# A four-layer graph stack on one core: last normalisation and squares moved to ScalarE, a bias on GpSimd, all orders written anew

## What is computed

```python
# layer 0: one-head attention, e = leaky_relu(s_i + t_j), softmax over neighbours, relu
# layer 1: eight heads of 16 features, e times a weight made of adj, softmax over neighbours, elu
# layer 2: mean over neighbours @ rel_weights[1] + x @ self_w.T + self_b, layernorm with gamma and beta, relu
# layer 3: four heads of 32 features, attention of Wh with itself
Wh = jnp.einsum('bsf,hfd->bhsd', features, W)
scores = jnp.einsum('bhsd,bhtd->bhst', Wh, Wh) / jnp.sqrt(jnp.float32(D))
scores = jnp.where(adj_matrix[:, None, :, :] > 0, scores, NEG_INF)
attn = jax.nn.softmax(scores, axis=-1)
h = jnp.einsum('bhst,bhtd->bhsd', attn, Wh)
# and the last step of the whole
x = _layernorm(x + _L3_gnn_ref(x, adj, L3_gnn_W), axis=-1)
```

## Time and profile before

| | us |
|---|---|
| median of 3 runs | 2479.86 (2475.13 to 2485.67) |
| profiled execution | 2479.01 |
| its span | 2477.2 |
| TensorE busy | 2241.7 (90%) |
| VectorE busy | 2223.9 (90%) |
| ScalarE busy | 1940.5 (78%) |
| GpSimd busy | 230.2 (9%) |

### The profile page before, as it was taken

How to read it: one execution, slowest core, us unless ns; L and a number is a source line. 1 busy time by engine, 2 the same in 40 slices (tenths; PEclk the granted TensorE clock), 3 DMA queues, 4 the chain that set the end, 5 groups by cost and what they waited for, 6 DMA issues and landing times.

```text
span 2477.2 us, 56662 instructions
## 1 busy us (share of the span) xinstructions
PE 2241.7 (90%) x23629; PEld 1505.8 (61%) x23629; DVE 2223.9 (90%) x4194; ACT 1940.5 (78%) x2152; POOL 230.2 (9%) x136
## 2 busy tenths in 40 slices
PE   4668999999999999999999999999999999998966
PEld 3567566575756657585665757566575756657331
DVE  3898899999999999999999999999999999999756
ACT  2758798787889878788987878798787979877724
POOL 0001010010101001010010101001010100101010
PEclk9789999999999999999999999999999999999979
DMA  7348034442614445251544525154452614405030
GB/s 132 88 90 163 13 96 86 109 98 69 112 48 125 86 103 104 69 112 44 129 86 103 104 67 114 44 129 86 96 111 54 125 45 126 90 27 95 10 60 9
DMA packets 262911, 214.20 MB, mean 86 GB/s; under 512 B 137664, under 2 KB 239168, under 8 KB 261696
## 3 DMA queue, kind: packets, MB, share of 16 engines
q0 software_dynamic: 71232, 74.98, 19.9%
q1 hardware_dynamic: 191424, 135.61, 19.5%
HBM read 151.78 MB, written 42.53 MB: 78 GB/s over the span
## 4 chain that ended last, share of the span: by engine, by line
PE 56%; DVE 20%; issue 11%; ACT 8%; DMA 4%; SPq 0%; POOL 0%; POOLq 0%; DVEq 0%; ACTq 0%
PE kp L1044 13%; PE kp L1027 10%; PE fp L852 9%; PE fp L923 7%; DVE weight L1550 7%; PE kp L1020 5%; ACT weight L1269 4%; DMA shared<-shared 2%; PE kp L904 2%; PE kp L973 2%; DVE bstat L1359 2%; DVE yb L1376 1%; PE fp L801 1%; DVE yb L1626 1%; PE kp L989 1%
## 5 line engine op out<-in xcount | busy, mean ns | idle before, releaser
L1221 ACT ACTIVATE ramp<-s1row,tbig 128x1024 bf16<-128x1024 f32 x854 | 912.7, 1147 | 28.0 <-DVE weight L1550 27.2
L1269 ACT ACTIVATE weight<-kp,shift 128x1024 f32<-128x1024 f32 x502 | 534.6, 1110 | 218.7 <-PE kp L1027 200.7
L1550 DVE TENSOR_TENSOR weight<-ramp,AT 128x2048 bf16<-128x2048 bf16 x512 | 609.0, 1218 | 45.8 <-PE fp L923 32.2
L1044 PE MATMUL kp<-weight,w 128*33 128x512 f32 x2048 | 487.0, 599 | 16.1 <-DVE weight L1688 9.4
L923 PEld LDWEIGHTS fp<-vh_parts,weight 128*128 128x128 bf16 x8192 | 393.2, 98 | 104.5 <-DVE weight L1550 56.3
L923 PE MATMUL fp<-vh_parts,weight 128*128 128x102 bf16 x8192 | 427.0, 209 | 32.7 <-DVE weight L1550 21.5
L1688 DVE SCALAR_TENSOR_TENSOR weight<-AT,weight 128x1024 f32<-128x1024 bf16 x272 | 321.3, 1218 | 35.4 <-ACT weight L1269 35.1
L1027 PE MATMUL kp<-shared 32*128 32x512 f32 x2008 | 295.6, 645 | 22.2 <-ACT weight L1269 19.3
L1044 PEld LDWEIGHTS kp<-weight,w 128*33 128x33 f32 x2048 | 100.2, 110 | 335.1 <-issue 233.1
L852 PEld LDWEIGHTS fp<-features,weight 128*128 128x128 f32 x1920 | 218.4, 193 | 39.2 <-issue 38.4
L852 PE MATMUL fp<-features,weight 128*128 128x129 f32 x1920 | 223.8, 278 | 14.4 <-DVE weight L1460 13.7
(11 more groups left out here) (202 smaller groups left out, 2606.0 us busy)
## 6 DMA issues: line engine op xcount, KB each, us to landing
s1row<-s_rows_dram SPq DMA_DIRECT2D x128, 512.0 KB, 4.1
AT<-minus POOLq DMA_DIRECT2D x16, 2048.0 KB, 18.4
adj_bf_dram<-in_adj_dram POOLq DMA_DIRECT2D x15, 2048.0 KB, 12.5
x<-in_x_dram SPq DMA_DIRECT2D x16, 512.0 KB, 5.0
xfT<-s_row_dram SPq DMA_DIRECT2D x16, 512.0 KB, 4.4
shared<-shared SPq DMA_DIRECT2D x32, 256.0 KB, 3.5
out_dram<-elu SPq DMA_DIRECT2D x16, 512.0 KB, 3.2
elu<-x POOLq DMA_DIRECT2D x15, 512.0 KB, 5.3
```

The costliest lines, as they stand in the source:

```text
L1044: last = pe.matmul(kp[side(h), 0, :], w3[:, (2 * J + x) * H3 + h, :], weight3[:, w % P_RING, x * HALF:(x + 1) * HALF], start=(J == 0 and x ...
L1221: act.activation(ramp[:, u % R_RING, :], s1row[:, h % S_RING, :], ACT.Relu, bias=tbig1[:, jt, h:h + 1], scale=BIG).then_inc(ramp_ready, 1)
L1269: act.activation(weight3[:, w % P_RING, :], score_banks(b, w).rearrange("p a n -> p (a n)"), ACT.Exp, bias=shift3[:, h:h + 1], scale=ROOT) ...
L1550: dve.tensor_tensor(edges[:, u % B_RING:u % B_RING + 2, :], ramp[:, u % R_RING:u % R_RING + 2, :], AT[:, third, jt:jt + 2, :], ALU.min).th ...
```

## The change

Three edits and a new set of orders:
1. `layer3_normalise` leaves VectorE's program and enters ScalarE's: eight Identity activations of 128x128, `rstd * x + shift`.
2. That needs a shift, -mean * rstd: `rstd_tail` on GpSimd waits for its own power and multiplies it by the negative mean (row 0 of `tsmall`) into row 6, under a new signal.
3. `squares3` is made by ScalarE straight from PSUM, behind the copy of `w3` and ahead of the signal for VectorE.
4. All tables have new numbers.

```diff
             def rstd_tail(b):
                 rstd(tvar_ready, trstd_ready, tsmall, b, 0)
+                pool.wait_ge(trstd_ready.sem, trstd_ready.of(b))
+                pool.tensor_tensor(tsmall[:, 6, :], tsmall[:, 0, :], tsmall[:, 5, :], ALU.mult) \
+                    .then_inc(tshift_ready.sem, 1)
@@ ScalarE
             def layer3_project(b):
                 act.wait_ge(w3_made.sem, w3_made.of(b))
                 src = kp[:, 3:5, :].rearrange("p a (b o) -> p (a b) o", o=O3)
-                copy(w3[:, :, 0:O3], src).then_inc(w3_ready.sem, 1)
+                copy(w3[:, :, 0:O3], src)
+                act.activation(squares3, src, ACT.Square).then_inc(w3_ready.sem, 1)
...
+            def layer3_normalise(b):
+                act.wait_ge(tshift_ready.sem, tshift_ready.of(b))
+                for t in range(T):
+                    last = act.activation(x4[:, t, :], x4[:, t, :], ACT.Identity, bias=tsmall[:, 6, t:t + 1],
+                                          scale=tsmall[:, 5, t:t + 1])
+                last.then_inc(x4_ready.sem, 1)
@@ VectorE
             def layer3_lengths(b):
                 dve.wait_ge(w3_ready.sem, w3_ready.of(b))
-                dve.tensor_tensor(squares3, w3[:, :, 0:O3], w3[:, :, 0:O3], ALU.mult).then_inc(back.sem, 1)
-                dve.wait_ge(back.sem, back.step())
                 dve.tensor_reduce(q3[:], squares3, AX_X, ALU.add).then_inc(back.sem, 1)
...
-            def layer3_normalise(b):
-                dve.wait_ge(trstd_ready.sem, trstd_ready.of(b))
-                normalise(x4, x4, tsmall, x4_ready.sem)
@@ ON_POOL, sections 1 and 2 to 14
-            (dict(adjacency=3, mask3=0, residual3=-1, rstd0=4, rstd1=5, rstd2=1, rstd3=2, rstd_tail=-1),),
-            (dict(adjacency=6, mask3=1, residual3=3, rstd0=5, rstd1=7, rstd2=0, rstd3=2, rstd_tail=4),),
+            (dict(adjacency=4, mask3=0, residual3=-1, rstd0=3, rstd1=5, rstd2=1, rstd3=2, rstd_tail=-1),),
+            (dict(adjacency=2, mask3=1, residual3=4, rstd0=6, rstd1=7, rstd2=0, rstd3=3, rstd_tail=5),),
@@ ON_SP, sections 2 to 14
-            (dict(adjacency=0, far=5, out=10, sources=[2, 3, 4, 7, 9], sources_ahead=[12, 13, 14], spread_row=8,
-                 store_row=6, store_sources=11, x=1),),
+            (dict(adjacency=1, far=8, out=10, sources=[2, 3, 4, 5, 6], sources_ahead=[12, 13, 14], spread_row=9,
+                 store_row=7, store_sources=11, x=0),),
```

More of the change, by code:

```diff
@@ L443, in graph_stack @@
[L443 to L456, removed]
@@ new lines, in graph_stack @@
+            (dict(affine2=18, columns1=[81, 82], cut1=[83, 84], cut1_third=[89, 90], divide1=69, elu1=73, finish0=70,
+                 finish1=59, finish3=-1, head1=[7, 12, 21, 27, 39, 46, 51, 58], lengths3=31, low2=88, masked3=[-1, -1,
+                 -1, -1, 57, -1, 63, -1, 71, -1, 75, 78, 80, 85, 86, -1], maxima1=77, maxima3=33, maximum0=49,
+                 most0=40, norm0=72, norm1=76, norm3=25, out2=14, prepare=-1, ramps=[-1, -1, -1, -1, 4, -1, -1, -1, 9,
+                 -1, -1, -1, -1, -1, -1, -1, -1, -1, -1, -1, -1, 30, -1, -1, 37, -1, -1, 44, -1, -1, -1, -1],
+                 relu2=22, rest2=87, shift0=54, shift3=34, shifts1=79, stats2=15, stats3=-1, top0=38, top1=74,
+                 unit0=[60, 61, 62, 64, 65, 66, 67, 68], unit1=[0, 1, 2, 3, 5, 6, 8, 10, 11, 13, 16, 17, 19, 20, 23,
+                 24, 26, 28, 29, 32, 35, 36, 41, 42, 43, 45, 47, 48, 52, 53, 55, 56], z0=50),),
@@ new lines, in graph_stack @@
+            (dict(affine2=21, columns1=[83, 84], cut1=[86, 87], cut1_third=[91, 92], divide1=71, elu1=75, finish0=72,
+                 finish1=64, finish3=25, head1=[7, 13, 19, 29, 36, 50, 54, 60], lengths3=35, low2=90, masked3=[-1, -1,
+                 -1, -1, 59, -1, 68, -1, 73, -1, 76, 79, 82, 85, 88, -1], maxima1=80, maxima3=37, maximum0=46,
+                 most0=30, norm0=74, norm1=78, norm3=27, out2=15, prepare=-1, ramps=[-1, -1, -1, -1, 2, -1, -1, -1, 9,
+                 -1, -1, -1, -1, -1, -1, -1, -1, -1, -1, -1, -1, 34, -1, -1, 43, -1, -1, 48, -1, -1, -1, -1],
+                 relu2=22, rest2=89, shift0=49, shift3=39, shifts1=81, stats2=18, stats3=52, top0=28, top1=77,
+                 unit0=[61, 62, 63, 65, 66, 67, 69, 70], unit1=[0, 1, 3, 4, 5, 6, 8, 10, 11, 12, 14, 16, 17, 20, 23,
+                 24, 26, 31, 32, 33, 38, 40, 41, 42, 44, 45, 51, 53, 55, 56, 57, 58], z0=47),),
@@ L580, in graph_stack @@
         ]
         ON_POOL = [
[L582 to L587 removed]
+            (dict(adjacency=1, mask3=-1, residual3=-1, rstd0=0, rstd1=-1, rstd2=-1, rstd3=-1, rstd_tail=-1),),
@@ new lines, in graph_stack @@
+            (dict(adjacency=0, mask3=-1, residual3=-1, rstd0=1, rstd1=2, rstd2=-1, rstd3=-1, rstd_tail=-1),),
+            (dict(adjacency=4, mask3=0, residual3=-1, rstd0=3, rstd1=5, rstd2=1, rstd3=2, rstd_tail=-1),),
+            (dict(adjacency=2, mask3=1, residual3=4, rstd0=6, rstd1=7, rstd2=0, rstd3=3, rstd_tail=5),),
+            (dict(adjacency=-1, mask3=1, residual3=3, rstd0=-1, rstd1=5, rstd2=0, rstd3=2, rstd_tail=4),
+                 dict(adjacency=-1, mask3=7, residual3=9, rstd0=-1, rstd1=-1, rstd2=6, rstd3=8, rstd_tail=10),
@@ L1306, in step @@
                         layer3_out(k, g)
+                if m is not None and s == at["tail3"]:
+                    layer3_normalise(m)
                 for w in range(U3):
```

219 lines of the change are left out of this document (107 added, 112 removed).

## The result

The changed kernel takes 2640.6 us (2638.1 to 2645.0) against 2478.6 for the kernel before on the same chip: 1.065 times as long, interval 1.064 to 1.067. The sign was forecast, the size was not: 162 us more where 35 were expected. The profiled execution of after has a span of 2639.6 us, that of before 2477.2.

A forecast was written before the change was run, and what follows sets the result against it. Bound: a 145.0 us loop through TensorE (95.6), VectorE (37.7) and hand-over (11.7), TensorE idling 7. Twelve periods of +2.9 (+34.8), +0.55, −2, +1.7: together +35 on 2479.9, 2514 us; own range 2490 to 2540, 8 in 10 2452 to 2532.

The forecast's parts named there:

- The adjacency load, +3.0 a period: Load moved behind the mask on GpSimd's queue delays the wT copy and scores: +3.0 us, hand-over's 0.65 included.
- the single contended spread: Traced spread issued 1.6 us behind a load: 12.7 us against median 4.1, landing 0.7 after the load; model for the copy.
- My upper case, +5: Upper bound of the load term: head 7's spread and the copy must still move afterwards, or the mask is slower.
- Squares, "by themselves they give nothing", with +0.35 on the hand-over: Taking squares off VectorE wins nothing; on ScalarE, ahead of the wT copy, they add 1.02 − 0.69 = +0.35 us.
- Tail normalisation, +0.6: Eight activations among ScalarE's exponentials, 3.2 us, delay layer-0 units behind them: +0.6 us a period, bounds 0 and +1.5.
- The order, −0.4 and −0.3: VectorE's part (37.7 us), same set in both tables: −0.4 us from starting earlier, −0.3 from fewer waits for exponentials.
- Period 1, −2: The load leaves its place beside the contended spread in period 1: −2 us, bounds 0 and −5.
- period 14, +0.55: Period without an adjacency load: +0.65 + 0.6 − 0.4 − 0.3 = +0.55 us.
- the end, +1.7: Kernel's end: normalisation 3.3 us on ScalarE for 2.14, plus 0.5 for GpSimd's product: +1.7, bounds 0.6 and 3.7.
- The load costs something: Against the rival that the moved load costs nothing: 2486 us, or 2479 with 0.5 a period won; chance 0.22.
- ScalarE loads one table: Against the rival that Square makes ScalarE swap function tables, 2.6 us a batch on the hand-over: 2525 to 2555; chance 0.03.
- VectorE's relief: Rival: 3.3 us less VectorE work cuts TensorE's waits by 2.0 a period: 2450 us, ceiling 2437; chance 0.22.

The follow-up runs named there:

- the queue run: Only the hand-over's DMAs, nothing computed, issued at the changed kernel's spacing and with parts left out: the copy takes 3.4 us alone, 12.6 inside a load.
- load_back_2: Changed kernel, adjacency untransposed, with GpSimd's adjacency load back behind rstd0 in the steady sections: 2537.8 us (1.024).
- the control after: Changed kernel with a plain instead of a transposing adjacency DMA (adjacency untransposed), nothing else changed: 2635.3 us (1.063).
- tail_alone: Kernel before, adjacency untransposed, with only the last layer's normalisation moved to ScalarE and its bias product to GpSimd: 2488.0 us (1.004).
- both_edits: Kernel before, adjacency untransposed, with squares and last normalisation both moved to ScalarE, every other order entry as before: 2521.3 us (1.017).
- the control before: Kernel before with a plain instead of a transposing adjacency DMA (adjacency untransposed), nothing else changed: 2474.3 us (0.998).
- no_squares: Kernel before, adjacency untransposed, with VectorE's squares multiplication left out, so it sums w, and nothing added: 2502.8 us (1.010).
- squares_held: squares_alone with VectorE's multiplication put back, so ScalarE and VectorE both compute the squares: 2496.6 us (1.007).
- squares_alone: Kernel before, adjacency untransposed, orders untouched, with only the squares moved from VectorE to ScalarE, written from PSUM: 2499.5 us (1.009).

## Why the prediction failed, step by step

**The adjacency load, +3.0 a period.** This is the term that failed; it measures 157.09 − 148.78 = 8.3. The steps up to it held. I had the copy leave 24.2 us behind the mask's issue (1237.9 to 1262.1): it left 25.3 behind (1317.52 to 1342.80). I had the load land 30.7 us behind it (1268.6), and it landed 30.9 behind. What failed is "By that the `wT` copy lands" 0.7 us after the load. From the single contended spread I took that a held transfer lands with the load. In the trace of after the load lands at 1348.4, the spreads of heads 6 and 7 at 1350.3 and 1354.2, the residual at 1353.3, and the halves of the copy at 1353.5 and 1355.4, up to 7.0 behind the load: all that the load had held back then moves at once. That spread had been alone, and the queue run has the same: 1.2 us behind the load with nothing else ahead of the copy, 6.3 with two spreads. My upper case, +5, had named it ("must still move afterwards") and was still too low.

The Trainium skill (DMA: Bandwidth & Descriptors, section Queues, rings and completion order), as the prediction cited it, says that rings are served in turn, a whole packet at a time. The queue runs agree in kind: 3.4 us to 12.6.

**The clock was in no term.** Between `load_back_2` and the control after, 8.6 us more wait for the copy (10.3 a time against 1.7) come with 4.3 us more of lost clock. Part of the latter lies in the wait itself and costs nothing, so the interval grows by 8.3 and not by the sum. For the small shifts it is most of the loss.

**Squares, "by themselves they give nothing", with +0.35 on the hand-over.** Half right. The hand-over grew by 0.1: the Square fills most of the 0.69 us for which ScalarE waited, and an activation here starts 0.1 us before the one ahead ends. But the relief of VectorE moved 0.5 us of wait from the q step to the scores, the late half-copies added 0.5 more, and the clock fell behind that wait in 10 of 12 periods: +2.2 a period.

**Tail normalisation, +0.6.** `tail_alone`: +0.57. The number agrees, partly by luck: half of it is lost clock (1.14 against 0.85), which was in no term. Eight Identity instructions take 3.18 us at the end and 3.1 in the chain of a period; 3.2 was forecast.

**The order, −0.4 and −0.3.** Wrong in sign: `load_back_2` has T 148.78 and `both_edits` 147.68, so the new orders outside GpSimd's load cost +1.1. The step "both tables hold the same set" is true of the list and not of its length. The affine (`yb<-yb,bsmall`) lies in VectorE's part. Its rows in the chain that ended last, before, then after:

```profile
1239.77 2.23 DVE yb L1376 x8
```

```profile
1317.90 3.99 DVE yb L1392 x8
```

In the new table it starts 0.3 us behind the mask's issue, while GpSimd is busy issuing for 3.2 us (shown above); before, two edge products came between and it started 2.6 us behind. Four of its eight instructions take 1.3 to 1.5 us instead of 0.33. The edge products that ran beside the same issue before kept their 1.22 us. The affine takes 4.06 us in every kernel with the new VectorE order (`load_back_2`, where the load is elsewhere, included) and 2.30 in every one with the old: 1.8 us of a 37.7 us part, and most of VectorE's missing relief. No run moved the affine alone, so that it makes up the 1.1 is argued and not shown. A new wait for `qdiag`, 1.0 us, takes the place of the 1.6 for `qmax`; others are new in layer 0: 0.8 for `xfT`, 0.7 for `st` (at `top0`, counted as 0.3), and 0.25 before its units, as forecast.

**Period 1, −2; period 14, +0.55; the end, +1.7.** Measured +4.4, +4.1 and +5.4. In period 1 `both_edits`, whose load stands in its old place there, is as long (154.8), so the load isn't needed for it. Period 14 has no load but all the rest, so the +4.1 repeats what the edits and the orders cost. At the end the product takes 0.20 us where 0.5 was taken, and the normalisation 3.18 for 2.14: +1.2 of 5.4 on the last chain. The rest is the last batches' exponentials behind the normalisation: VectorE's wait for them from 2270 us on grows in `tail_alone`, shown behind the control before.

```profile
DVE weight L1688 <- ACT weight L1269: 26.4, 21, 3.7
```

```profile
DVE weight L1714 <- ACT weight L1286: 34.9, 19, 5.4
```

**The rivals.** The load costs something (101 and 98 us). ScalarE loads one table, as before. VectorE's relief (1.3 us a period) bought nothing, and `no_squares` shows it at its purest.

In sum, from the control before to the control after: the two edits 47 us (25 for the squares, 14 for the normalisation, 8 only together), the other orders 16, the load 98. The steps follow one another from run to run, so they add up to the 161 by construction; each carries the spread of its runs, a few us.

## What to carry to other kernels

When a large transfer is moved, follow everything that it holds back, not only the one transfer that you care for: what was held moves at once afterwards and delays the latest issued most. On an engine that is close to the bound, weigh how idle time is cut up, not only its sum: work taken from a neighbour can turn two short waits into one long one, and the clock behind it costs more than the work was worth. When a table of orders is exchanged, exchange it whole or not at all; one engine's old section can starve another's new one. And look at what runs beside an issue of GpSimd: the same eight instructions took 2.3 us in one place and 4.1 in another.

## What was not expected of the hardware

A load of 2 MB from DRAM to DRAM makes a 3.4 us copy between partitions take 12.6 us, and in eight pieces still 10.4; with the residual beside it, that takes 22 to 23 us instead of 10.9 (single landings of the queue run). Eight VectorE instructions of 128x128 (a tile, less a mean, times a root) take 4.06 us beside GpSimd's issue of the mask and 2.1 without one; an edge product of 128x2048 in bf16 keeps its 1.22 us beside it. TensorE's granted clock fell to 0.50 behind single waits of 2.3 us (matmuls of one stretch 2.88 us for 1.60) and stayed at 1.00 behind 1.78. The length of one wait doesn't settle it: it fell in all 12 hand-overs of `load_back_2` behind 1.6 to 2.9 us, with 1.0 just ahead, and in none of the control's, where one has 1.9 with 1.4 ahead; in `squares_held` it fell in 9 of 12 behind the same 2.35. What decides stays open. Open too is why every third period of `squares_alone` has its second half-copy land at 5.8 to 6.2 us behind the first one's issue instead of 4.3. Each of these periods, and no other of that kernel, has a 16 KB packet of instruction loading in the copy's time; but four of the control's have one too, with 4.3 to 4.9 us.
